# From the fourth block on, x is also loaded transposed and the queries come from three rounded products

## The reference

```
xn  = (x - mean(x)) / sqrt(var(x) + 1e-5)
q   = xn @ wq + bq;  k = ctx @ wk + bk;  v = ctx @ wv + bv      # 16 heads of 8
o   = softmax_over_8((q k^T / sqrt(8)) v);   x1 = x + o @ wo.T + bo
t   = rms(layernorm(x1)) * norm_w
w   = top-2 of softmax(t @ gate.T), normalised
h1e = t @ w1.T + 2 (t @ a1e.T) @ b1e.T ;  h3e likewise
out = x1 + sum over the two e of  w_e * ((silu(h1e)*h3e) @ w2.T + 2 ((silu(h1e)*h3e) @ a2e.T) @ b2e.T)
```

## Time and profile before

| | |
|---|---|
| median of 3 runs | 297.6 us (297.27 to 298.34) |
| profiled execution, first to last instruction | 296.7 us |
| PE busy | 287.4 us, 97% |
| DVE / ACT / POOL busy | 221.4 (75%) / 187.5 (63%) / 187.0 (63%) |
| mean granted TensorE clock | 0.992 of full speed |

### The profile page before, as it was taken

How to read it: one execution, slowest core, us unless ns; L and a number is a source line. 1 busy time by engine, 2 the same in 40 slices (tenths; PEclk the granted TensorE clock), 3 DMA queues, 4 the chain that set the end, 5 groups by cost and what they waited for, 6 DMA issues and landing times. The chain is left out here.

```text
span 296.7 us, 4518 instructions
## 1 busy us (share of the span) xinstructions
PE 287.4 (97%) x1487; PEld 238.4 (80%) x1487; DVE 221.4 (75%) x607; ACT 187.5 (63%) x310; POOL 187.0 (63%) x186
## 2 busy tenths in 40 slices
PE   8779999999999999999999999999999999999995
PEld 6557888878888888888888888888888887878874
DVE  3878986995689658894589765895579965795295
ACT  1467967674945966757755868459656658655532
POOL 3375599288970889419990589608982389518930
PEclk9979999999999999999999999999999999999999
DMA  5720020200220021200211011200012000200002
GB/s 147 287 66 9 0 73 1 72 1 11 97 73 0 0 72 38 71 1 2 71 50 60 0 49 59 71 0 2 1 37 73 0 0 35 75 1 0 0 2 71
DMA packets 7225, 12.45 MB, mean 42 GB/s; under 512 B 1825, under 2 KB 3234, under 8 KB 7202
## 3 DMA queue, kind: packets, MB, share of 16 engines
q1 hardware_dynamic: 6768, 11.77, 12.0%
q10 hardware_dynamic: 434, 0.39, 0.4%
HBM read 10.03 MB, written 2.13 MB: 41 GB/s over the span
## 5 line engine op out<-in xcount | busy, mean ns | idle before, releaser
L989 ACT ACTIVATE silu<-h_ps 128x512 f32<-128x512 f32 x64 | 37.4, 596 | 31.4 <-PE h_ps L641 29.8
L1639 POOL TENSOR_TENSOR um_lo<-umf,um_hi 128x1024 fp32r<-128x1024 f32 x7 | 16.9, 2414 | 60.5 <-ACT um_hi L981 60.5
L641 PE MATMUL h_ps<-um_hi,b_hi 128*128 128x512 f32 x128 | 51.4, 401 | 0.0
L641 PE MATMUL h_ps<-um_lo,b_hi 128*128 128x512 f32 x128 | 50.3, 393 | 0.5 <-DVE um_lo L1309 0.5
L641 PE MATMUL h_ps<-um_hi,b_lo 128*128 128x512 f32 x128 | 49.9, 390 | 0.0
L1322 DVE TENSOR_TENSOR act_first<-silu,h_ps 128x512 f32<-128x512 f32 x32 | 21.4, 680 | 20.9 <-ACT silu L989 16.1
L1322 DVE TENSOR_TENSOR act_second<-silu,h_ps 128x512 f32<-128x512 f32 x32 | 21.7, 679 | 16.6 <-PE h_ps L641 14.7
L1661 POOL TENSOR_TENSOR scaled<-act_second,ratio 128x512 f32<-128x512 f32 x24 | 31.5, 1313 | 1.3 <-DVE act_second L1322 1.3
L641 PEld LDWEIGHTS h_ps<-um_lo,b_hi 128*128 128x128 f32 x128 | 24.0, 188 | 6.9 <-DVE um_lo L1309 1.4
L981 ACT CAST um_hi<-umf 128x1024 fp32r<-128x1024 f32 x14 | 14.8, 1055 | 23.2 <-DVE umf L1303 22.2
L641 PEld LDWEIGHTS h_ps<-um_hi,b_lo 128*128 128x128 f32 x128 | 24.1, 188 | 4.5
(11 more groups left out here) (278 smaller groups left out, 789.2 us busy)
## 6 DMA issues: line engine op xcount, KB each, us to landing
chosen<-choice_dram SPq DMA_DIRECT2D x7, 512.0 KB, 3.6
x_in<-in_x_dram SPq DMA_DIRECT2D x7, 256.0 KB, 2.9
...
act_second<-in_hidden_w_dram SPq DMA_DIRECT2D x1, 512.0 KB, 4.1
act_second<-in_lora_w_dram SPq DMA_DIRECT2D x1, 512.0 KB, 5.6
v_parts<-in_down_w_dram SPq DMA_DIRECT2D x1, 512.0 KB, 5.3
ctx_in<-in_ctx_t_dram ACTq DMA_DIRECT2D x2, 128.0 KB, 3.2
```

The source lines that it names most:

```text
L641: mm = nc.tensor.matmul((h1_ps, h3_ps)[s][n % 2][:], b13[w][:, s, c * P:(c + 1) * P], um[k][m][:, s, :], start=False, stop=(i == 2), skip_ ...
L989: nc.scalar.activation(silu[:, n % SILU_RING, :], h1_ps[n % 2][:], ACT.Silu).then_inc(silu_done.sem, 1)
L1639: nc.gpsimd.tensor_tensor(um[1][1][:], umf[1][:], as_f32(um[1][0][:]), ALU.subtract)\
```

## The change

For blocks 3 to 7 (`TURNED = 3`), x is loaded a second time, already transposed (`x_t`), into the buffer that held `xn_t`. Centring moves into the weights: a 128x128 centring matrix is loaded at the start, PE multiplies it with `wq` once, and the product is split into `wq_hi` and `wq_lo`. The reciprocal deviation, one number per token, must lie along the free axis now: POOL makes it (`turned_rstd`, two small instructions), SP writes it to DRAM and reads it back into all partitions (`spread_rstd`), POOL multiplies the transposed x by it (`scale_x`), ACT and DVE split the result (`x_high`, `x_low`), and PE forms the queries by three fp32r products. `normal_x`, `turn_x`, `x_turned` and plain `queries` fall away for these blocks.

On SP, two new helpers and their place in the loop:

```diff
+            def load_xt(n):
+                if n == TURNED:
+                    sp.wait_ge(q_mm.sem, q_mm.of(n - 1))
+                else:
+                    sp.wait_ge(xs_done, turned(n - 1))
+                sp.dma_start(xt_in, x_t[:, n * BLK:(n + 1) * BLK]).then_inc(xt_loaded, 16)
...
+            def spread_rstd(n):
+                sp.wait_ge(rstd_done.sem, rstd_done.of(n))
+                sp.dma_start(rstd_dram[n % 2].rearrange("(p c) -> p c", c=TILES), rstd[:]).then_inc(rstd_out, 16)
+                sp.wait_ge(rstd_out, turned(n, 16))
+                if n > TURNED:
+                    sp.wait_ge(xs_done, turned(n - 1))
+                sp.dma_start(rstd_rows[:], rstd_dram[n % 2].partition_broadcast(P)).then_inc(rstd_in, 16)
...
                     load_ctx(b + 3)
+                    load_xt(b + 3)
...
                     spread_choice(b + 1)
+                if b + 3 < BLOCKS:
+                    spread_rstd(b + 3)
```

On PE:

```diff
+            def center_queries():
+                pe.wait_ge(center_in, 16)
+                nc.tensor.matmul(h1_ps[0][:, 0:P], center_sb, wq_sb, start=True, stop=True).then_inc(wqc_mm, 1)
...
+            def turned_queries(n):
+                if n == TURNED:
+                    pe.wait_ge(wq_lo_ready, 1)
+                pe.wait_ge(o_t_done.sem, o_t_done.of(n - 3))
+                pe.wait_ge(xs_hi_done, turned(n))
+                pe.wait_ge(xs_lo_done, turned(n))
+                for i, (w, m) in enumerate(TERMS):
+                    mm = nc.tensor.matmul(odd_ps[:], wq_split[w], xs_split[m][:], start=(i == 0), stop=(i == 2))
+                mm.then_inc(q_mm.sem, 1)
...
             keys_values_ahead(1, 1)
+            center_queries()
             turn_x(1)
...
                 if early:
-                    turn_x(b + 2)
                     keys_values(b + 2, 0)
...
                 if early:
-                    queries(b + 2)
+                    turned_queries(b + 2)
```

On ACT:

```diff
+            def centered_queries():
+                sc.wait_ge(wqc_mm, 1)
+                nc.scalar.copy(wqc_sb, h1_ps[0][:, 0:P]).then_inc(wqc_done, 1)
...
+            def x_high(n):
+                sc.wait_ge(xs_done, turned(n))
+                sc.wait_ge(q_mm.sem, q_mm.of(n - 1))
+                nc.scalar.copy(xs_split[0][:], xs).then_inc(xs_hi_done, 1)
...
             normal_x(1)
+            centered_queries()
...
                 if early:
-                    normal_x(b + 2)
+                    x_high(b + 2)
...
-                if early:
-                    x_turned(b + 2)
```

On DVE:

```diff
+            def x_low(n):
+                ve.wait_ge(xs_hi_done, turned(n))
+                nc.vector.tensor_tensor(xs_split[1][:], xs, as_f32(xs_split[0][:]), ALU.subtract).then_inc(xs_lo_done, 1)
...
                 early = b + 2 < BLOCKS
+                if early:
+                    x_low(b + 2)
                 act_step(b, 0)
```

On POOL:

```diff
+            def turned_rstd(n):
+                pool.wait_ge(mv_done.sem, mv_done.of(n))
+                if n == TURNED:
+                    pool.wait_ge(xn_done.sem, xn_done.of(n - 1))
+                else:
+                    pool.wait_ge(rstd_out, turned(n - 1, 16))
+                nc.gpsimd.tensor_tensor(var_eps[:], mv[:, :, 1], eps_ln[:], ALU.add).then_inc(var_done.sem, 1)
+                pool.wait_ge(var_done.sem, var_done.of(n))
+                nc.gpsimd.tensor_tensor(rstd[:], var_eps[:], minus_half[:], ALU.pow).then_inc(rstd_done.sem, 1)
...
+            def scale_x(n):
+                pool.wait_ge(xt_loaded, turned(n, 16))
+                pool.wait_ge(rstd_in, turned(n, 16))
+                if n == TURNED:
+                    pool.wait_ge(xn_t_mm.sem, xn_t_mm.of(n - 1))
+                else:
+                    pool.wait_ge(xs_lo_done, turned(n - 1))
+                nc.gpsimd.tensor_tensor(tile4(xs), tile4(xt_in), rstd_rows[:].rearrange("q (p c) -> q c p", c=TILES),
+                                        ALU.mult).then_inc(xs_done, 1)
...
                 if b + 3 < BLOCKS:
-                    rstd_x(b + 3)
+                    turned_rstd(b + 3)
                 choice_words(b + 1)
                 z_low(b)
                 scale_step(b, 2)
+                if b + 3 < BLOCKS:
+                    scale_x(b + 3)
                 um_low(b + 1)
                 if early:
```

More of the change, by code:

```diff
@@ L42 @@
 AHEAD = 2
+TURNED = 3
 INDICES = TOP * TILES
@@ L86, in upto, with build_program @@
     return None if i is WHOLE else i + 1
-def build_program(nc: bass.Bass, x, ctx_t, wkv, query_w, mask_w, attn_w, rows, hidden_w, lora_w, down_w, b2, row_expert, out):
+def build_program(nc: bass.Bass, x, x_t, center, ctx_t, wkv, query_w, mask_w, attn_w, rows, hidden_w, lora_w, down_w, b2, row_expert, out):
     with ExitStack() as ctx:
@@ L199, in build_program @@
         ones = sb("ones", [1, P])
+        rstd_rows = sb("rstd_rows", [P, BLK])
+        xs_split = [sb("xs_hi", [P, BLK], F32R), sb("xs_lo", [P, BLK], F32R)]
+        wq_split = [wq_hi[:], wq_lo[:]]
+        xt_in, xs = xn_t[:], flat(xn)
+        center_sb, wqc_sb = o_t[:, 0:P], o_t[:, P:2 * P]
         h1_ps = [psum("h1_ps0"), psum("h1_ps1")]
@@ L258, in build_program @@
         ctx_first = [sem("ctx_first0"), sem("ctx_first1")]
+        center_in = sem("center_in")
+        wqc_mm = sem("wqc_mm")
+        wqc_done = sem("wqc_done")
+        wq_hi_ready = sem("wq_hi_ready")
+        wq_lo_ready = sem("wq_lo_ready")
         const_pool = sem("const_pool")
@@ L278, in build_program @@
         xn_done = signal("xn_done", first=2)
+        xt_loaded = sem("xt_loaded")
+        rstd_out = sem("rstd_out")
+        rstd_in = sem("rstd_in")
+        xs_done = sem("xs_done")
+        xs_hi_done = sem("xs_hi_done")
+        xs_lo_done = sem("xs_lo_done")
         ctx_hi_done = signal("ctx_hi_done")
@@ L390, in build_program, with turned @@
         PARTS = (slice(0, 2), slice(2, 3), slice(3, 4))
+        def turned(n, k=1):
+            return k * (n - TURNED + 1)
         LAST = BLOCKS - 1
@@ L1709, in _ @@
             scale_step(0, 2)
+            turned_rstd(3)
+            centered_low()
             ctx_low(3)
-            rstd_x(3)
+            scale_x(3)
             um_low(1)
```

34 lines of the change are left out of this document (24 added, 10 removed).

## The result

The changed kernel takes 303.0 us (median of 4 runs, 300.3 to 304.8), the kernel before 298.0 us beside it (4 runs, 297.3 to 298.8): ratio 1.0148, interval 1.0106 to 1.0191, 5.1 us slower. The forecast was 302.6. The number held; the way to it was only half the one that the prediction described. The profiled execution has a span of 302.9 us, 6.2 more than before; it is the longest of the four.

The account below looks back on a forecast made before the run. PE was taken to bound the loop, with almost no slack at the turn's head (DVE's um_lo) and at turn_tok. Terms 0.6 + 0.55 + 4.2 - 0.4 = +4.95 us on 297.6 gave 302.6 us, range 297.5 to 306.5.

Parts of the forecast that it names:

- The start, +0.6: Program start: centring product and its copy delay ACT's cast b_hi, tok_t and the first hidden product; +0.6 us (0 to 0.7).
- scale_x(3), +0.55: Ahead of turn 1: POOL's scale_x(3) ends at 63.1, so DVE's um_lo, due at 62.40, waits 0.55 us (0.05 to 1.05).
- scale_x in four turns, 4 x 1.04: Ends of turns 1 to 4: POOL's scale_x, 126.2 to 128.0, delays DVE's second z_lo 1.04 us; 4.2 us altogether (2.2 to 6.2).
- I take the middle, 2.5: Ends of turns 1 to 4: reading rstd back, 256 KB, takes 2.5 us, so it lands at 126.1 (125.0 to 127.2).
- I let it land at 123.6: Ends of turns 1 to 4: the write of rstd, queued behind chosen landing at 123.47, lands at 123.6.
- the first rival: Ends of turns 1 to 4: rstd lands after about 127.5, scale_x runs beside umf without loss; 298.3 us, chance 0.20.
- x_low, -0.08 a turn: Starts of turns 1 to 5: POOL loses 0.42 us to x_low, so a turn keeps 0.08 of 0.53 us; -0.4 altogether.
- PE's saving: Blocks 3 to 7: PE saves 0.53 us per block without turn_x and plain fp32 queries; 2.65 us if all comes through.
- PE's saving comes through: Rival: DVE and POOL hinder each other less, turn_tok's chain has more give, only the start costs; 295.5 us, chance 0.12.

Follow-up runs that it names:

- `scale_x` held back: Changed kernel, with scale_x of turns 1 to 4 also waiting until DVE's second mask is done: 302.3 us, ratio 1.0135 to the kernel before.
- `den` on ACT: Changed kernel, with block 1's den made by ACT and DVE's reciprocal left behind um_low(1): 301.1 us, ratio 1.0128 to the kernel before.
- `x_low` in the gap: Changed kernel with scale_x behind the second mask, first_weight(1) and centring moved, plus x_low behind act_step(b,1), waiting for POOL's v: 297.0 us, ratio 0.9969.
- the two experiments on it: Changed kernel, once with first_weight(1) moved behind act_step(1,1), 302.0 us; once with block 1's den on ACT, reciprocal left in place, 301.1 us.

## Why the number held and the steps did not

**The start, +0.6: near in size, but with no term for the clock.** Reckoned from the first turn of heads, 0.89 in the profiled execution and 0.48 with `scale_x` held back (9.89 for 9.41), both with a fall of the clock as in the earlier trace rows. Where it did not fall, the same steps took 8.74 us (`den` on ACT), 0.67 less than the kernel before with its fall. So what the start costs in one execution hangs on the clock as much as on the added steps. The centring product took 0.64 us at the lower clock, 0.38 at the higher; 0.35 had been assumed.

**scale_x(3), +0.55: the term was half as large, and what stood behind it was missed.** DVE's `um_lo` lost 0.27 us, not 0.55: `scale_x` took 1.58 us, not 1.8, and ended 0.40 us behind `um_lo`'s start (62.84 + 1.58 against 64.02) instead of 0.70. But the step asked only what the delayed operation costs, and not what it now comes behind. `den` had 0.10 us to spare against POOL's `um_lo`; the prediction did not look, for it took only operations with two SBUF inputs as able to collide, and `den` has one and is 0.17 us long. That is +2.2 us, the largest single loss. Nor had the split of the centred weights a price; `wq_lo` on POOL cost DVE's chain another 0.27.

**scale_x in four turns, 4 x 1.04: the price was nearly right, the landing was not.** The step that failed is the landing of the read: "I take the middle, 2.5", between 1.44 and 3.6 us. Until `scale_x` starts it takes 3.5 to 4.1 us, at that upper bound or above it. "I let it land at 123.6" for the write held: put into the time of the kernel before (counted from the choice at 118.43), the read was issued at 123.5 to 124.6 in the four turns, at 123.8 in turn 1. So `scale_x` comes at 127.3 in turns 1 and 4, at 127.6 in turn 2 and at 128.8 in turn 3, not at 126.1, and the first rival begins "after about 127.5". Forecast and rival were both true, turn by turn: two turns paid 1.25 us (the mask waited 1.20; `scale_x` is 1.57 us long, not 1.8), two paid nothing. The step held up was the second mask, not `z_lo`. Whether POOL would have got in at the first mask, as the prediction assumed, no run shows.

**x_low, -0.08 a turn: right in mechanism, 0.1 us too hopeful in size.** The two stretches that hold an `x_low` and no collision are 0.06 and 0.07 us longer than before, and 0.03 to 0.06 with `scale_x` held back. `ctx_lo` lost 0.46 us (0.42 said), and PE kept 0.06 us at the keys and values (0.12 said), which start 0.10 us behind the end of `ctx_lo` (142.12); in the kernel before they started 0.61 behind it. The kernel with `x_low` in the gap shows that its place took PE's saving: elsewhere 0.42 to 0.51 us a turn come back. It does not separate the wait of POOL's `ctx_lo` from that of DVE's steps behind `x_low`. The prediction's rival "PE's saving comes through" put the decision at `turn_tok`, with `q_t` 0.4 us earlier; with `x_low` in the gap both came earlier by that much against the kernel before (`turn_tok` 28.49 us behind the choice for 28.88), but `turn_tok` follows PE's own order and does not stop for `q_t`.

**The sum.** +0.6, +0.55, +4.2, -0.4 were forecast; 1.27 (the start), 2.28 (the head of turn 1), 2.5 (the four turns) and 0.14 are found in the profiled execution, 6.2 together; the median of the runs rose by 5.1. The term of the four turns was too large by 1.7 us and the one of turn 1's head too small by 1.7. That these two cancelled is chance: without `den` the changed kernel would have come out at 301 to 302 us (the two experiments on it), with four collisions near 307 (estimated from 302.3 without any and 4 x 1.25).

**What the rows of before could tell.** The loss of `den` stood in the trace of the kernel before, at the end of turn 6. DVE, then POOL, kernel before:

```profile
267.01 1.33 DVE L1280 TENSOR_SCALAR den<-e_gap 128x4 f32<-128x4 f32 x1
...
265.91 2.41 POOL L1639 TENSOR_TENSOR um_lo<-umf,um_hi 128x1024 fp32r<-128x1024 f32 x1 [9.54 <-ACT um_hi L981]
```

Seven of its eight `den` take 0.17 to 0.23 us; this one began 1.10 us behind POOL's `um_lo` and ended with it, at 268.3. The rule of "SBUF — State Buffer" of the Trainium skill, section "SBUF: two separate sides", lists, besides operations with two SBUF inputs, DVE operations in a two-port mode as holders of the lock. The `den` of 1.33 and 2.36 us, with one input, beside POOL's `um_lo`, and the undisturbed reciprocal in its place, agree with that; that `den` ran in such a mode no run here shows by itself. The prediction had used only the half of the rule on two inputs, which the second mask (2.38 us for 1.18) bears out.

The price of the step of four numbers the trace of before could not tell. The page "GPSIMD Engine Reference" of the Trainium skill, section "Performance pitfalls for Q7 kernels", asks half more for a step above 8 bytes; measured are 1.57 against 1.29 us, 22% more, with one of two inputs stepped, and for this operation the measurement decides.
